# A decoder block in float32: score turns into two banks, slots whose registers are loaded once, and the memory's rows minus their mean on ScalarE

## The chip, the cores and the metric

One core of one Trainium2 chip runs the whole program in one launch. The metric is the device time of that launch in microseconds (us), lower is better. Its engines are TensorE (PE), VectorE (DVE), ScalarE (ACT), GpSimd (POOL) and SyncE (SP). Each runs its own instructions in order, and they wait for each other by semaphores.

## The reference

Two layers over `x` of 16 x 128 x 256, all float32; only the parts that the change touches are spelled out.

```python
x = x + L0_attn(layernorm(x))        # 16 heads of 16: softmax(q k^T / 4) v, then w_o and b_o
x = x + L0_conv(ctx, ctx, layernorm(x), ssm_kernel, D)   # a long convolution per head
x = x + L0_experts(layernorm(x))     # one of 8 experts per row (top 1), and a shared expert
x = x + L1_attn(layernorm(x))        # 16 heads, full attention within each 128 rows
x = x + L1_memory(layernorm(x), ctx, mask)
x = x + L1_ffn(layernorm(x))         # two quantised linear layers

def _layernorm(x, eps=1e-05):
    m = mean(x); v = var(x)
    return (x - m) / sqrt(v + eps)

def L1_memory(h, mem, mask):
    scores = einsum('bsd,bmd->bsm', h, mem) / sqrt(256)
    attn = softmax(where(mask, scores, -1e30))
    return where(any(mask), einsum('bsm,bmd->bsd', attn, mem), 0)

def L0_experts(h, ...):
    e, w = top_1(h @ router.T)
    return sigmoid(w) * glu(h, w1[e], v1[e], w2[e]) + glu(h, shared...)
```

## The kernel before

The rows are cut into 16 tiles of 128 rows x 256 columns, one per batch entry. The stages follow one another: attention of layer 0 with the first steps of the convolution beside it, the convolution, the experts, attention of layer 1 with the memory's cross-attention beside it, and the feed-forward. Each engine's program is written out by hand with counting semaphores; there is no scheduler, so the order in the code is the order on the engine. A function `pipeline` runs a stage's body for t = 0, 1, ..., with the first six t written out, the rest in a loop of two tiles per turn, and the tail written out. What belongs to another stage is put in by `follow(engine, ..., step)`, and the functions `on_act` and `on_dve` of the memory are called so.

**Attention, one body.** TensorE's eight banks are four for the scores `S` (which Q, K and V also use in turn), `T` (bank 4), `O` (bank 5), `M` (bank 6) and `X` (bank 7). For tile t TensorE makes the scores (`pe_scores`, L313) of all 16 heads into `S`; VectorE reduces the first 8 heads to their maximum (L545, "max 0") and subtracts it (L551, "sub 0"), then the same for the other 8 (max 1, sub 1); ScalarE takes the exponential (L468). The probabilities are turned in four groups of four heads (`pe_turn`, L321, turns 0 to 3): four transposes into `T`, and ScalarE copies the bank out (`act_copy`, L473, copies 0 to 3). As `T` is one bank, turn r waits for copy r-1 (semaphore `pT`). Then come P times V (`pe_pv`, L331, into `O`), ScalarE's copy of it, its transposition back into `O` (`pe_o_turn`, L339), and on VectorE the reciprocal of the sums (L568) and the scaled result (L574, "att", semaphore `att`). Layer 0 also turns that result (`pe_att_turn`, L379) and multiplies it by `w_o` (`pe_out`, L386) into `M`; VectorE adds it to x (L581), after GpSimd added the bias to x (L636).

TensorE's order in one body is: scores of t, turn 1 of t-1, (layer 0: the result of t-2), the normed rows of t+1 turned (L250), what follows from convolution or memory, turn 2, (layer 0: `pe_out`), turn 3, Q and K of t+1 (L349, L359), P times V of t-1, turn 0 of t, V of t+1 (L369), `pe_o_turn`. Q may not start before sub 0 has read the scores' banks. The scores wait for ScalarE's copy of V (L485).

**A layer norm.** VectorE takes the statistics of the rows (L216, L221), GpSimd makes 1/sqrt(var + eps) from them (L230, L233), VectorE writes the normed rows (L242, `front_xn`), and TensorE turns them (L250). In layer 0 two of them run per body: that of the next attention tile, and that of the convolution. In layer 1 the second is the memory's.

**The experts.** Rows are sorted by expert; 23 slots of up to 128 sorted rows each belong to one expert. The routing leaves the expert of each slot in a row of SBUF (`expert_of`). The shared expert's second product is L1057, added by VectorE in L1065. Then 12 fill-in products keep TensorE busy (`keep_busy`, L71), and `slots` runs `pe_slot` for each slot: it loads the expert numbers of its own slot and of the slot before from SBUF into registers of TensorE (L1105), turns the rows of the next slot (L1101), turns the hidden layer (L1116) and multiplies by the weights of the expert (L1124 gate and up, L1132 down). The first six slots are written out, the rest lie in a loop.

## Time and profile before

| | us |
|---|---|
| the three runs | 732.82, 733.7, 3345.06 |
| their median | 733.7 |
| the profiled execution | 735.13 |
| its span, first to last instruction | 733.2 |

In the profiled execution TensorE is busy 620.5 us (85% of the span), VectorE 531.9 (73%), ScalarE 386.5 (53%), GpSimd 323.0 (44%), and the mean granted clock of TensorE is 0.956 of full speed. The run of 3345.06 us stands alone and is left aside. The stages as they lie in the trace are: attention of layer 0 until about 175 us, the convolution's products until about 250, the routing, the experts' slots from about 316 to 400, attention of layer 1 from about 411 to 590, the feed-forward to the end. A row of the trace gives the start and the length of an instruction or of several alike in a row; in square brackets stands how long the engine had been idle and what it had waited for.

### The profile page before, as it was taken

Reading aid. Unit: us, or ns where it says so; the run is one execution under the profiler, and the core shown is the slowest. Engines: PE = TensorE matmul, PEld = TensorE weight load, DVE = VectorE, ACT = ScalarE, POOL = GpSimd, SP = SyncE. Lnnn points to the kernel's source line nnn. Section 1 sums busy time; section 2 is a strip of 40 time slices with the busy share of each in tenths; the row PEclk is TensorE's granted clock in tenths of the full one; section 3 lists DMA queues with packets and bytes.
Section 4 is the critical chain, followed back from the end, with each engine's and each line's share of the span. In section 5 each row is a group of like instructions: output and inputs, shape, how many; then the busy total and the mean of one; then the engine's idle time right before and its main releaser. Section 6 shows DMA issues by size and latency. Waiting matters only on the chain.

```text
span 733.2 us, 16347 instructions
## 1 busy us (share of the span) xinstructions
PE 620.5 (85%) x4645; PEld 463.8 (63%) x4647; DVE 531.9 (73%) x1217; ACT 386.5 (53%) x796; POOL 323.0 (44%) x672
## 2 busy tenths in 40 slices
PE   6899999987889899988999777999999667827776
PEld 5787888864444475566777566888887433315554
DVE  4688888873999986325222678899998458779994
ACT  2567777662111123234232264777776438779993
POOL 1223222233999642711111554333333258667772
PEclk9899999999999999999999998999999669969999
DMA  8901400000343100274541213000000000000011
GB/s 302 415 35 31 167 0 0 0 1 6 53 57 57 29 1 0 102 235 132 152 135 50 59 36 109 2 1 0 1 0 1 2 0 1 0 0 1 14 46 57
DMA packets 27342, 42.00 MB, mean 57 GB/s; under 512 B 3520, under 2 KB 22608, under 8 KB 26400
## 3 DMA queue, kind: packets, MB, share of 16 engines
q1 hardware_dynamic: 23808, 31.14, 14.4%
q0 software_dynamic: 3488, 10.28, 4.1%
q8 instruction: 25, 0.41, 0.2%
q14 instruction: 21, 0.17, 0.1%
HBM read 31.15 MB, written 10.26 MB: 56 GB/s over the span
## 4 chain that ended last, share of the span: by engine, by line
PE 61%; issue 12%; ACT 9%; DVE 8%; POOL 5%; DMA 3%; SPq 1%; DVEq 0%; POOLq 0%; ACTq 0%
PE ps L321 9%; PE ps L1124 5%; PE ps L349 5%; PE ps L331 4%; PE ps L313 4%; PE ps L359 4%; PE ps L369 4%; PE ps L713 4%; PE ps L1132 2%; PE ps L386 2%; PE ps L339 2%; POOL sorted_x L1185 2%; ACT wide L473 2%; ACT work L1718 2%; ACT wide L1689 2%
## 5 line engine op out<-in xcount | busy, mean ns | idle before, releaser
L230 POOL TENSOR_TENSOR var_eps<-mv,powers 128x1 f32<-128x1 f32 x80 | 16.8, 209 | 215.2 <-DVE mv L221 215.0
L473 ACT COPY wide<-ps 128x512 f32<-128x512 f32 x128 | 75.1, 587 | 60.9 <-PE ps L321 60.9
L321 PE MATMUL ps<-ident,work 128*128 128x128 f32 x512 | 84.0, 288 | 10.0 <-ACT wide L473 9.0
L545 DVE TENSOR_REDUCE work<-ps 128x8 f32<-128x1024 f32 x64 | 77.9, 1218 | 12.4 <-PE ps L313 12.4
L321 PEld LDWEIGHTS ps<-ident,work 128*128 128x128 f32 x512 | 56.4, 144 | 36.5 <-issue 29.3
L551 DVE TENSOR_TENSOR work<-ps,work 128x1024 f32<-128x1024 f32 x64 | 77.9, 1217 | 0.8 <-issue 0.2
L713 PE MATMUL ps<-ctxT,small 128*128 128x512 f32 (+1 forms) x192 | 65.7, 493 | 8.0 <-DVE ctx_sb L819 3.1
L468 ACT ACTIVATE work<-work 128x1024 f32<-128x1024 f32 x64 | 67.9, 1061 | 8.1 <-DVE work L551 7.5
L713 PEld LDWEIGHTS ps<-ctxT,small 128*128 128x128 f32 x192 | 35.3, 190 | 37.7 <-issue 28.0
L1158 DVE TENSOR_TENSOR work<-work,ps 128x256 f32<-128x256 f32 x23 | 9.7, 421 | 56.6 <-ACT work L1152 56.6
L349 PE MATMUL ps<-xnT,w_qkv 128*128 128x128 f32 x256 | 38.3, 298 | 11.5 <-DVE work L551 9.8
L233 POOL TENSOR_TENSOR rstd<-var_eps,powers 128x1 f32<-128x1 f32 x80 | 44.6, 557 | 6.3
L1168 POOL DMA_DIRECT2D sorted_y<-work x23 | 13.5, 588 | 75.1 <-DVE work L1163 75.1
L1736 PE MATMUL ps<-work,wide 128*128 128x128 f32 x256 | 32.9, 284 | 15.0 <-DVE work L1782 15.0
L216 DVE BATCH_NORM_STATS2 bn<-x 128x6 f32<-128x256 f32 (+1 forms) x96 | 40.5, 422 | 5.2 <-DMA x<-in_x 2.6
L1124 PE MATMUL ps<-wide,work 128*128 x184 | 43.9, 381 | 0.0
L313 PE MATMUL ps<-wide,work 32*128 32x256 f32 x512 | 36.7, 399 | 8.0 <-ACT work L485 6.4
L349 PEld LDWEIGHTS ps<-xnT,w_qkv 128*128 128x128 f32 x256 | 34.3, 208 | 13.4 <-issue 11.5
L833 DVE TENSOR_REDUCE wide<-ctx_sb 128x1024 f32 x32 | 39.0, 1220 | 4.5
L751 ACT COPY xnT<-ps 128x256 f32<-128x256 f32 x32 | 11.8, 373 | 56.9 <-PE ps L713 56.9
L1736 PEld LDWEIGHTS ps<-work,wide 128*128 128x128 f32 x256 | 31.5, 201 | 15.6 <-issue 15.4
L331 PE MATMUL ps<-wide,work 128*32 128x128 f32 x1024 | 35.7, 281 | 2.7 <-ACT wide L473 2.7
(207 smaller groups left out, 1556.5 us busy)
## 6 DMA issues: line engine op xcount, KB each, us to landing
wide<-in_expert_gu SPq DMA_DIRECT2D x1, 4096.0 KB, 20.8
small<-hank SPq DMA_DIRECT2D x32, 128.0 KB, 3.8
sorted_x<-small POOLq DMA_DIRECT2D x1, 2944.0 KB, 12.5
work<-sorted_x SPq DMA_DIRECT2D x23, 128.0 KB, 2.1
sorted_y<-work POOLq DMA_DIRECT2D x23, 128.0 KB, 2.4
xn_all<-in_ctx_rev_t SPq DMA_DIRECT2D x1, 2048.0 KB, 10.7
wide<-in_expert_d SPq DMA_DIRECT2D x1, 2048.0 KB, 25.3
xn_all<-in_ffn_w SPq DMA_DIRECT2D x2, 1024.0 KB, 6.3
```

The lines of the kernel that those rows point to most:

```text
L233: pool.tensor_tensor(f.rstd_v[u], f.var_eps[u], powers[:, 0:1], ALU.pow).then_inc(f.rstd, 1)
L313: mm = pe.matmul(S[i][:, c * 2 * P:(c + 1) * 2 * P], qT[u][rows, c, :], kTm[u][rows, c, :], start=True, stop=True, skip_group_check=True)
L321: mm = pe.transpose(T[:, h * P:(h + 1) * P], prob[r][:, h * P:(h + 1) * P], ident)
L331: mm = pe.matmul(O[VW * k:VW * k + VW, r * P:(r + 1) * P], va[u][:, GH * r + k, :], probT[r][:, k * P:(k + 1) * P], start=True, stop=True, ...
L349: mm = pe.matmul(Q[:, j * P:(j + 1) * P], w[:, c, j * P:(j + 1) * P], xT(c), start=(c == 0), stop=(c == KT - 1), skip_group_check=True)
L468: act.activation(prob2[g], prob2[g], ACT.Exp, scale=ATT_SCALE).then_inc(s["exp"], 1)
L473: act.copy(probT[r], T).then_inc(s["pT"], 1)
L545: dve.tensor_reduce(mxs[:, 8 * g:8 * g + 8], S2[g], AX.X, ALU.max).then_inc(s["mx"], 1)
L551: dve.tensor_tensor(prob2[g].rearrange("p (h k) -> p h k", k=P), S2[g], m.unsqueeze(2).broadcast_to([P, 2 * GH, P]), ALU.subtract).then_in ...
L713: mm = pe.matmul(ps[4 * u + o][:, 0:n], toep[u][:, c, lt * P:(lt + 1) * P], kv[u][:, c, half * UPPER:half * UPPER + n], start=(c == 1 - lt ...
L1124: mm = pe.matmul(ps[2 * k + u][:, 0:NI], xsT[u][:, c * P:(c + 1) * P], w_ex_gu[:, c, ds(expert * (2 * NI) + k * NI, NI)], start=(c == 0), ...
L1736: pe.matmul(TB2[1 - u][:, c * P:(c + 1) * P], y[:, c * P:(c + 1) * P], diag[1 - u], start=(c % 4 == 0), stop=False, skip_group_check=True)
```

## The change

1. **Two banks for turns.** `T` becomes a pair, bank 4 and `O`. Turns 0 and 2 go to bank 4, turns 1 and 3 to `O`. A turn now waits for the copy of the turn two before it, and turn 1 waits instead for the `att` of the tile before, which reads `O`. V of t+1 moves ahead of turn 0 of t. In layer 0, turn 3 comes right behind turn 2, ahead of `pe_out`. In layer 1, turns 2 and 3 come together ahead of the memory's readout and scores; the memory's own turned probabilities go to columns 128 to 255 of `M`, with two waits that this needs, and the wait for `att` ahead of them goes.
2. **VectorE's order.** In layer 1 (and, as the orders below show, in layer 0, where the convolution's normed rows are a step 3 too) step 3 and the memory's maximum come ahead of the reciprocal and `att`.
3. **The memory's norm.** `front_xn` of the memory leaves VectorE. ScalarE writes the mean minus x (Identity, bias the mean, scale -1, step "apart"), behind copy 0. GpSimd makes `nscale`, the reciprocal root times -1/16, and VectorE's score step multiplies by it where it multiplied by 1/16.
4. **The slots.** TensorE loads all 23 expert numbers once, ahead of `keep_busy`, and the 23 slots are all written out.

```diff
-            S, T, O, M, X = ps[0:4], ps[4], ps[5], ps[6], ps[7]
+            S, O, M, X = ps[0:4], ps[5], ps[6], ps[7]
+            T = [ps[4], O]
             def pe_turn(pe, t, u, r):
                 pe.wait_ge(s["exp"], 2 * B + 2 * t + r // 2 + 1)
-                wait(pe, s["pT"], 4 * B + 4 * t + r)
+                if r == 1:
+                    wait(pe, s["att"], B + t)
+                else:
+                    wait(pe, s["pT"], 4 * B + 4 * t + r - 1)
...
-                if there(t):
-                    pe_turn(pe, t, u, 0)
                 if there(t + 1):
                     pe_v(pe, t + 1, 1 - u)
+                if there(t):
+                    pe_turn(pe, t, u, 0)
...
-                wait(pe, s["att"], B + upto(t - 1))
-                follow("pe", pe, t, u, 0, X=X[:, D:2 * D], KO=turned_to(t))
+                follow("pe", pe, t, u, 0, X=X[:, D:2 * D], KO=M)
                 if there(t - 1):
                     pe_turn(pe, t - 1, 1 - u, 2)
+                    pe_turn(pe, t - 1, 1 - u, 3)
                 follow("pe", pe, t, u, 3, KO=M)
                 follow("pe", pe, t, u, 1, KO=M)
-                if there(t - 1):
-                    pe_turn(pe, t - 1, 1 - u, 3)
...
+                follow("act", act, t, u, "apart ready")
                 if there(t):
                     act_copy(act, t, 0)
+                follow("act", act, t, u, "apart")
...
                 follow("dve", dve, t, u, 2, KO=M)
+                follow("dve", dve, t, u, 3, KO=M)
+                follow("dve", dve, t, u, "2 end", KO=M)
                 if there(t - 1):
                     dve_att(dve, t - 1)
-                follow("dve", dve, t, u, "2 end", KO=M)
-                follow("dve", dve, t, u, 3, KO=M)
...
-                load = lambda t: pe.value_load(expert_of[0:1, ds(t, 1)], min_val=0, max_val=NE - 1)
                 if in_range(t):
-                    expert = load(t)
+                    expert = experts[t]
...
                 pe.wait_ge(s["expert"], 1)
+                experts = nc.values_load_multi_w_load_instructions(
+                    expert_of[0:1, :], engines=[mybir.EngineType.PE], min_val=0, max_val=NE - 1)[1]
                 pe.wait_ge(s["sh_h"], 10)
                 pe.wait_ge(s["x_shared"], 2 + DOWN_FIRST)
                 keep_busy(pe, ps[5], ident, 12)
                 pe_turn_slot(pe, 0, 0, 0)
-                slots("pe", pe, pe_slot, 1, 1)
+                for t in range(NS + 1):
+                    pe_slot(pe, t, t % 2, t // 2, experts)
+                    if 2 <= t < 6:
+                        beside_slots("pe", pe, t - 2)
...
                     if there(p):
                         pe.wait_ge(s["exp"], p + 1)
                         wait(pe, s["pT"], p)
-                        pe.transpose(KO, prob[u], ident).then_inc(s["pT_ps"], 1)
+                        wait(pe, s["masked"], upto(t - 3))
+                        wait(pe, s["x_new"], p)
+                        pe.transpose(KO[:, P:2 * P], prob[u], ident).then_inc(s["pT_ps"], 1)
...
+                n = t - 2
+                if step == "apart ready" and there(n):
+                    act.wait_ge(f.stats, f.base + n + 1)
+                    wait(act, f.xnT_ps, f.base + n - 1)
+                if step == "apart" and there(n):
+                    act.activation(slot2(f.xn_buf, u, D), tile_of(x, n), ACT.Identity, bias=f.mean[u],
+                                   scale=-1.0).then_inc(f.xn, 1)
...
-                    dve.scalar_tensor_tensor(sc[1 - u], KO[:, 0:P], float(D) ** -0.5,
+                    dve.scalar_tensor_tensor(sc[1 - u], KO[:, 0:P], nscale[1 - u],
...
-                if step == 3 and there(n):
-                    front_xn(dve, f, n, u)
...
+                    eng.wait_ge(f.rstd, f.base + t - 1)
+                    wait(eng, s["masked"], t - 3)
+                    eng.tensor_tensor(nscale[u], f.rstd_v[u], c_nroot, ALU.mult).then_inc(s["nscale"], 1)
```

TensorE, loop of layer 0's attention, the second half of a body: P times V (L331; behind the change L335), turn 0 (L321; L325), V (L369; L373) and `pe_o_turn` (L339; L343). Before:

```order
L331 MATMUL ps<-wide,work 32x128 [waits att_att,att_v_sb,att_pT]
L331 MATMUL ps<-wide,work 32x128 x15
L318 REGISTER_ALU
L321 MATMUL ps<-ident,work 128x128 [waits att_pT,att_exp]
L321 MATMUL ps<-ident,work 128x128 x3
L369 MATMUL ps<-w_qkv,xnT 128x256 [waits att_sub,att_v_sb]
L369 MATMUL ps<-w_qkv,xnT 128x256
L339 MATMUL ps<-ident,work 128x128 [waits att_oT]
L339 MATMUL ps<-ident,work 128x128 x3
```

With the change:

```order
L335 MATMUL ps<-wide,work 32x128 [waits att_att,att_v_sb,att_pT]
L335 MATMUL ps<-wide,work 32x128 x15
L373 MATMUL ps<-w_qkv,xnT 128x256 [waits att_sub,att_v_sb]
L373 MATMUL ps<-w_qkv,xnT 128x256
L319 REGISTER_ALU
L43 REGISTER_ALU [waits att_exp]
L325 MATMUL ps<-ident,work 128x128 [waits att_pT]
L325 MATMUL ps<-ident,work 128x128 x3
L343 MATMUL ps<-ident,work 128x128 [waits att_oT]
L343 MATMUL ps<-ident,work 128x128 x3
```

V has moved ahead of turn 0, and `pe_o_turn` now follows turn 0 directly.

TensorE, the same loop, the middle of a body: turns 2 and 3 (L321; L325) and `pe_out` (L386; L390). Before:

```order
L43 REGISTER_ALU [waits att_exp]
L321 MATMUL ps<-ident,work 128x128 [waits att_pT]
L321 MATMUL ps<-ident,work 128x128 x3
L386 MATMUL ps<-w_o,work 128x256 [waits att_x_new,att_attT]
L386 MATMUL ps<-w_o,work 128x256
L43 REGISTER_ALU [waits att_exp]
L321 MATMUL ps<-ident,work 128x128 [waits att_pT]
L321 MATMUL ps<-ident,work 128x128 x3
```

With the change:

```order
L43 REGISTER_ALU [waits att_exp]
L325 MATMUL ps<-ident,work 128x128 [waits att_pT]
L325 MATMUL ps<-ident,work 128x128 x3
L43 REGISTER_ALU [waits att_exp]
L325 MATMUL ps<-ident,work 128x128 [waits att_pT]
L325 MATMUL ps<-ident,work 128x128 x3
L390 MATMUL ps<-w_o,work 128x256 [waits att_x_new,att_attT]
L390 MATMUL ps<-w_o,work 128x256
```

The two turns now stand in a row, and `pe_out` behind them.

VectorE, the same loop, the end of a body: the x update (L581; L580), the normed rows of the next attention tile (first L242) and of the convolution (second L242), reciprocal (L568; L567) and `att` (L574; L573). Before:

```order
L581 TENSOR_TENSOR x<-x,ps 128x256
L242 TENSOR_SCALAR xn<-x,mv,rstd 128x256 [waits front0_xnT_ps,front0_rstd]
L568 RECIPROCAL work<-ps 128x16 [waits att_ot_ps]
L574 TENSOR_TENSOR work<-ps,work 128x256 [waits att_attT_ps,att_rsum]
L242 TENSOR_SCALAR work<-x,mv,rstd 128x256 [waits front1_xnT_ps,front1_rstd]
```

With the change:

```order
L580 TENSOR_TENSOR x<-x,ps 128x256
L242 TENSOR_SCALAR xn<-x,mv,rstd 128x256 [waits front0_xnT_ps,front0_rstd]
L242 TENSOR_SCALAR work<-x,mv,rstd 128x256 [waits front1_xnT_ps,front1_rstd]
L567 RECIPROCAL work<-ps 128x16 [waits att_ot_ps]
L573 TENSOR_TENSOR work<-ps,work 128x256 [waits att_attT_ps,att_rsum]
```

The convolution's normed rows now come ahead of the reciprocal and of `att`, straight behind the attention's.

TensorE, between the shared expert (L1057; L1056) and the first slot: fill-in products (L71), turned rows (L1101; L1100), register load (L1105; L1232). Before:

```order
L71 MATMUL ps<-ident 128x128 [waits moe_x_shared,moe_sh_h,moe_expert]
L71 MATMUL ps<-ident 128x128 x11
L1101 MATMUL ps<-ident,work 128x128 [waits moe_xs0]
L1101 MATMUL ps<-ident,work 128x128
L1105 TENSOR_LOAD small
L1105 ISA x2
L1101 MATMUL ps<-ident,work 128x128 [waits moe_xsT,moe_xs1]
L1101 MATMUL ps<-ident,work 128x128
```

With the change:

```order
L1056 MATMUL ps<-w_sh,work 128x256
L1232 TENSOR_LOAD small [waits moe_expert]
L1232 ISA x46
L71 MATMUL ps<-ident 128x128 [waits moe_x_shared,moe_sh_h]
L71 MATMUL ps<-ident 128x128 x11
L1100 MATMUL ps<-ident,work 128x128 [waits moe_xs0]
L1100 MATMUL ps<-ident,work 128x128
```

All registers are now loaded, and 46 register instructions run, ahead of the fill-in products.

## Rows read from the trace of the kernel before

**Rows 1.** The page, part 4: the chain that ended last, by engine.
```profile
PE 61%; issue 12%; ACT 9%; DVE 8%; POOL 5%; DMA 3%; SPq 1%; DVEq 0%; POOLq 0%; ACTq 0%
```

**Rows 2.** Timeline, TensorE, a tile of layer 0 (start us, length us, operation, count).
```profile
90.59 1.15 PE L313 MATMUL ps<-wide,work 32*128 32x256 f32 x16 [0.21 <-ACT work L485]
...
93.00 0.65 PE L321 MATMUL ps<-ident,work 128*128 128x128 f32 x4
...
94.50 0.60 PE L321 MATMUL ps<-ident,work 128*128 128x128 f32 x4
94.93 1.06 PE L349 MATMUL ps<-xnT,w_qkv 128*128 128x128 f32 x8
...
99.18 0.60 PE L339 MATMUL ps<-ident,work 128*128 128x128 f32 x4
```

**Rows 3.** Timeline, VectorE, the same tile.
```profile
91.80 1.22 DVE L545 TENSOR_REDUCE work<-ps 128x8 f32<-128x1024 f32 x1 [0.34 <-PE ps L313]
...
93.28 1.21 DVE L551 TENSOR_TENSOR work<-ps,work 128x1024 f32<-128x1024 f32 x1
...
99.82 0.26 DVE L568 RECIPROCAL work<-ps 128x16 f32<-128x16 f32 x1 [0.70 <-PE ps L339]
...
100.45 0.40 DVE L242 TENSOR_SCALAR work<-x,mv,rstd 128x256 f32 x1
```

**Rows 4.** Timeline, ScalarE, then GpSimd, the same tile.
```profile
92.36 0.58 ACT L473 COPY wide<-ps 128x512 f32<-128x512 f32 x1 [1.52 <-PE ps L321]
...
99.22 0.73 POOL L636 TENSOR_TENSOR x<-x,row_bias 128x256 f32 x1
```

**Rows 5.** Timeline, TensorE: scores, tiles 1, 15 (layer 0); 4, 15 (layer 1).
```profile
24.55 1.15 PE L313 MATMUL ps<-wide,work 32*128 32x256 f32 x16 [0.66 <-ACT work L485]
...
156.47 1.15 PE L313 MATMUL ps<-wide,work 32*128 32x256 f32 x16 [0.23 <-ACT work L485]
...
460.99 1.15 PE L313 MATMUL ps<-wide,work 32*128 32x256 f32 x16 [0.23 <-ACT work L485]
...
563.39 0.93 PE L313 MATMUL ps<-wide,work 32*128 32x256 f32 x12 [0.23 <-ACT work L485]
```

**Rows 6.** Timeline, GpSimd and VectorE, in layer 0 and behind it.
```profile
62.27 0.74 POOL L636 TENSOR_TENSOR x<-x,row_bias 128x256 f32<-128x256 f32 x1
...
62.78 0.40 DVE L242 TENSOR_SCALAR work<-x,mv,rstd 128x256 f32<-128x256 f32 x1
...
165.50 1.24 DVE L242 TENSOR_SCALAR work<-x,mv,rstd 128x256 f32<-128x256 f32 x1
```

**Rows 7.** Line L1105, TensorE's queue, 334.4 to 336 us (ns min/median/max); timeline.
```profile
L1105 PEldq TENSOR_LOAD <-small x2: 296/304/313, 334.6 to 335.2; - x2
L1105 PEldq FUSED_REGOPS  x2: 146/148/151, 334.9 to 335.6; - x2
...
313.18 2.92 PE L71 MATMUL ps<-ident 128*128 128x128 f32 x24 [0.71 <-DVE x L1065]
...
335.97 0.30 PE L1101 MATMUL ps<-ident,work 128*128 128x128 f32 x1 [1.06 <-issue]
```

**Rows 8.** Timeline, TensorE: the slots.
```profile
347.53 1.92 PE L1124 MATMUL ps<-wide,work 128*128 x8
...
391.86 1.93 PE L1124 MATMUL ps<-wide,work 128*128 x8
...
394.99 1.93 PE L1124 MATMUL ps<-wide,work 128*128 x8
```

**Rows 9.** Busy us (count) PE, PEld, DVE, ACT, POOL; PEclk, DMA, GB/s.
```profile
440.00:442.50 2.50, 0.00 (x0) 0.00 (x0) 2.50 (x4) 0.04 (x2) 1.89 (x3) 0.50 0.73 234
442.50:446.00 3.50, 3.41 (x16) 3.44 (x16) 2.34 (x4) 2.36 (x4) 2.15 (x4) 0.50 0.93 352
```

**Rows 10.** Timeline, TensorE, behind layer 1's last tile.
```profile
575.40 1.09 PE L321 MATMUL ps<-ident,work 128*128 128x128 f32 x4 [1.13 <-ACT wide L473]
...
585.00 0.66 PE L250 MATMUL ps<-ident,work 128*128 128x128 f32 x2 [1.52 <-DVE work L242]
```

40 lines of the change are left out of this document (21 added, 19 removed).

## The prediction

> **What bounds the kernel now.** I read the chain of waits first. By engine its shares are TensorE 61%, issue 12%, ScalarE 9%, VectorE 8% [rows 1]: the span is set by TensorE for the most part, and what can be won is short waits of TensorE on the others. So next I read one tile of layer 0 on every engine. The scores start at 90.59, Q at 94.93, `pe_o_turn` at 99.18 and, after a wait of 0.21 for ScalarE's V copy, the next scores about 0.8 behind it [rows 2]. Three things hold TensorE up there. The scores wait for V. Turn 2 starts at 93.00 right behind copy 1, which runs from 92.36 for 0.58 [rows 2, 4]. And Q comes behind turn 3, which waits its turn behind `pe_out` and copy 2. The reader is to see that all are a few tenths; the tile takes 9.42 us (24.55 to 156.47 is 131.92 for 14 tiles), and in layer 1 9.31 (460.99 to 563.39 is 102.40 for 11) [rows 5].
>
> **Layer 0.** With two banks and the new order the three waits go, and I ask what is late next.
>
> *TensorE and sub 0.* Max 0 starts 1.21 behind the scores, sub 0 at 93.28 and ends at 94.49, so 3.90 behind the scores' start [rows 2, 3]. With 0.14 for the semaphore, Q can start at 4.04, against 4.34 now. TensorE's own work up to there is 4.34 less the two waits, about 0.3, so 4.05: the same. Q to `pe_o_turn` is 4.25 [rows 2] and only changes its order. `pe_o_turn` takes 0.43 before the next instruction can follow, as turn 3 does ahead of Q (94.50 to 94.93), plus 0.03. The sum is 4.05 + 4.25 + 0.46 = 8.76.
>
> *VectorE and GpSimd.* The attention's next normed rows are made late in the body, in step with GpSimd, which starts adding the bias (L636) at 99.22, when it has made the convolution's 1/sqrt; that is 7.42 behind max 0 at 91.80 [rows 3, 4]. Only now may the convolution's normed rows (L242) start, and the change puts them ahead of the reciprocal. They need 0.35 on the queue, reciprocal and `att` need 0.63 (99.82 to 100.45) [rows 3], so max 0 of the next tile may come 7.42 + 0.08 + 0.35 + 0.63 = 8.48 behind the last. Taken alone that is below 8.76. But L242 now starts with L636 beside it, where before it came when L636 was over. What this costs the rows bound from both sides: L242 at 62.78 had L636 (62.27, 0.74) beside it for half its time and took its usual 0.40; at 165.50, with GpSimd starting an addition at the same time, it took 1.24 [rows 6]. The nearest row is in between, as L242 would start some 0.1 into L636; I take half of the 0.84, 0.42, which gives 8.90, and keep 8.76 (cost hidden behind TensorE) and 9.32 for the range.
>
> So a tile takes 8.90 where it took 9.42, and 14 tiles save 7.3. The two ends of the stage have the same waits in smaller number, 1.1 together (an estimate: two tiles' worth of 0.52). Layer 0 gives **8.4** (bounds 14 x 0.10 = 1.4 and 16 x 0.66 = 10.6).
>
> The Trainium skill, GPSIMD Engine Reference, section Specifications, says that GpSimd shares its interfaces to SBUF with VectorE, and that the two get in each other's way where VectorE runs in a mode that uses both ports or reads two inputs from SBUF. By that rule taken hard, L242 would take its 1.24 here each time and the gain of layer 0 would be near its lower bound. The row at 165.50 agrees; the one at 62.78 shows no delay.
>
> The added wait of turn 1 for `att` stands with the scores of the next tile behind it: turn 1 comes 1.08 behind the scores' start, `att` about 0.1 before that by the sum above. I cost it at nothing; each tenth by which `att` is later costs a tenth per tile.
>
> **Layer 1.** The memory's normed rows leave VectorE (0.40 a tile) and go to ScalarE. There they stand behind copy 0, in a stretch where ScalarE has room: it is busy 53% of the span. The multiplication for `nscale` is one more small step of GpSimd. Here no L242 stands beside L636, so TensorE's sum of 8.76 should hold; turns 2 and 3 go ahead of the memory's products, and the wait for `att` is gone. 11 tiles save 11 x (9.31 - 8.76) = 6.1. The four tiles at the start of the layer have the same turns, 4 x 0.6 = 2.4. Behind the last tile TensorE waits 1.13 for a copy ahead of a turn at 575.40 and 1.52 for the normed rows at 585.00 [rows 10]. Two banks remove most of the first, ScalarE's earlier rows most of the second, and the rest of the tail has some smaller ones of the first kind: I take 3.3, from 1 to 4. Layer 1 gives **11.8** (7 to 13). The lower bound is that the tile stays bound by VectorE, whose work a tile lost only 0.40: 11 x 0.40 + 1 + 1.6.
>
> **The slots.** What goes: two loads per slot on TensorE's queue, each 0.30 for the load and 0.15 for the operation behind it [rows 7]. A slot takes 3.41 in the middle ((391.86 - 347.53) / 13), while the last, with no load of a next slot, takes 3.13 [rows 8]. Not all of the difference is the loads; I take 0.21 a slot for 13 slots, 2.7. The one place where the issue itself shows, 1.06 of idle ahead of 335.97 [rows 7], goes too, and some 0.3 elsewhere: 4.1 in all (1 to 5).
>
> What comes: one load and 23 pairs of register operations ahead of the fill-in products. In the trace two such pairs start 0.7 apart, 0.30 of it the load between them [rows 7]. So a pair needs 0.3 to 0.4, and no less than 0.15; 23 x 0.30 + 0.3 = 7.2, with ends at 3.8 and 9.7. TensorE ends its product at 312.47 (313.18 less 0.71), and its queue is free about one us earlier. The fill-in products now start at 318.5 in place of 313.18, 5.3 later; the first slot stands behind them, and nothing covers this. And the array is idle for 6 us. After a shorter idle time (440.00 to 442.50 has no product at all) the granted clock was 0.50 for the next 3.5 us of work [rows 9], which is the lower of the two levels, 1.2 GHz; the work of these 3.5 us takes twice its time, which loses 1.8. The prologue costs 7.1, from 2.3 (short operations, no fall of the clock) to 10.5. The slots lose **3.0** net.
>
> The Trainium skill, TensorE: Matmul & The Clock Gate, Part 1, says that an array left idle falls back to 1.2 GHz and needs sustained work to come back. The rows at 440.00 and 442.50 agree. If the clock didn't fall here, the sum would be 1.8 lower.
>
> **Sum.** 8.4 + 11.8 - 3.0 = 17.2 less. The profiled execution would take 735.13 - 17.2 = 717.9. The median of the runs shown is 1.4 below it, which gives 716.5; I say **717**.
>
> **Rivals.**
>
> 1. *The loads cost next to nothing.* If the register operations overlap the shared expert's last products, the slots gain 4 in place of losing 3, and the time is 716.5 - 7.1 = 709.5. For it: TensorE's queue runs ahead of the array. Against it: it can do so by one group of products only, and 0.15 is a measured duration of the operation.
> 2. *VectorE and GpSimd take the gain of layer 0.* L242 at the full 1.24, or `att` late for turn 1, holds the tile at 9.32. Layer 0 then gives 1.4 + 1, about 6 less: 722.5. With layer 1 at its lower bound too it is 727. For it: the row at 165.50, and that VectorE is busy 73% over the whole. Against it: the row at 62.78.
> 3. *Slower than before: the slots written out.* Their code is now a straight run on TensorE's queue with 23 different bodies. If each needed fetching as at 335.97, where the array sat idle 1.06 on issue behind new code [rows 7], 20 slots would cost 21, and the time would be 716.5 + 21, about 738. It decides against the change from 0.85 us per slot on. Against it: the first six slots are written out already, and issue shows once.
> 4. *The change doesn't do what it says.* Turns in two banks still wait, since ScalarE's copies come in the same order and Q waits for sub 0. Then the layers give 0.1 a tile, some 5 with the tail, and with the slots' loss the time is 731.
>
> **How the numbers follow.** My forecast, with its own range of 713 to 720, has 0.48; rival 1 has 0.12, rival 2 0.28, rival 3 0.04, rival 4 0.08. The range from 710 to 726 leaves out the last two and a part of the first two. About 2% is what a measurement of this kernel can tell from no change, so the border to "faster" is at 719.0. Below it lie rival 1 and most of the forecast's own range, 0.57; within 2% lie the rest of it, rivals 2 and 4, 0.38; slower is rival 3 and little else, 0.05.
>
> **What would show it.** In the profile after, the start of the scores of tile 1 to that of tile 15 in layer 0 should be about 124.6 in place of 131.9, with L242 at a mean between 0.4 and 0.8 us, and the wait ahead of the scores gone. In layer 1 the tile should take 8.8. Ahead of the slots the register operations should fill some 7 us, the fill-in products should start near 318.5 at a granted clock of 0.5 and last nearly 5 us; the slots should be 3.1 to 3.3 apart. I am wrong if the register operations run faster than 0.2 a pair, if L242 is never stretched, or always, or if a new wait for `att` stands ahead of turn 1.

## The result, and the profile after

| | before | with the change |
|---|---|---|
| median of 14 runs each, us | 734.48 | 728.98 |
| ratio to before | | 0.9925 (95% interval 0.9901 to 0.995) |
| profiled execution, its span, us | 735.13, 733.2 | 725.95, 724.3 |

The change gains 0.75%, 5.5 us, where 717 was predicted and 710 to 726 was the range. The run of 3345.06 us stays aside. The profiled execution of the changed kernel is one of the quickest of its 14, so its span is 8.9 lower than that of before; what follows reads where these 8.9 lie.

The page's chain of waits, by engine, reads now:

```profile
PE 56%; issue 15%; DVE 14%; ACT 7%; DMA 3%; POOL 3%; DVEq 1%; SPq 1%; POOLq 0%; ACTq 0%
```

VectorE has 14% of it where it had 8%, and issue 15% where it had 12% [rows 1]; both turn up again below. Next the starts of the scores in the timeline of TensorE (scores are L314 now), tiles 1 and 15 of layer 0, 4 and 15 of layer 1, to be held against [rows 5]:

```profile
20.80 0.93 PE L314 MATMUL ps<-wide,work 32*128 32x256 f32 x12 [0.23 <-ACT work L482]
...
146.91 1.15 PE L314 MATMUL ps<-wide,work 32*128 32x256 f32 x16
...
457.80 1.15 PE L314 MATMUL ps<-wide,work 32*128 32x256 f32 x16
...
556.23 1.14 PE L314 MATMUL ps<-wide,work 32*128 32x256 f32 x15
```

Layer 0: 20.80 to 146.91 is 126.11 for 14 tiles, 9.01 each, against 131.92. The waits on ScalarE ahead of the scores are gone. Layer 1: 98.43 for 11 tiles, 8.95 each, against 102.40. So the loops alone give 5.8 + 4.0.

The last products of the convolution, first before, then with the change, end at 250.80 and at 238.50:

```profile
246.67 4.13 PE L713 MATMUL ps<-ctxT,small 128*128 128x512 f32 x12 [0.19 <-POOL ctxT L773]
...
233.74 4.76 PE L712 MATMUL ps<-ctxT,small 128*128 128x256 f32 x14
```

Of these 12.3 the loop of layer 0 gives 5.8, and from the scores of tile 15 to the end of the convolution it is 2.7 less. The other 3.75 lie ahead of tile 1, and they are for the most part the clock's. TensorE waits 2.52 for sub 0 of tile 0 in both kernels, and its next eight products, Q of tile 1, take 2.05 before and 1.13 with the change:

```profile
17.73 2.05 PE L349 MATMUL ps<-xnT,w_qkv 128*128 128x128 f32 x8 [2.52 <-DVE work L551]
...
16.64 1.13 PE L353 MATMUL ps<-xnT,w_qkv 128*128 128x128 f32 x8 [2.52 <-DVE work L550]
```

From 18 to 20 us the granted clock is 0.50 before, its lower level of 1.2 GHz, and 1.00 with the change. It doesn't go with the kernel: in another profile of the changed kernel (changed_again, below) it is 0.50 there too, and tile 1 starts at 23.89.

Then the stretch ahead of the slots. The first rows are the operations of the new line L1232 on TensorE's queue (ns min/median/max, first and last start), then the timeline:

```profile
L1232 PEldq FUSED_REGOPS  x23: 146/146/165, 305.4 to 311.7; - x23
...
L1232 PEldq TENSOR_LOAD <-small x1: 6018/6018/6018, 299.3 to 299.3; - x1
...
294.82 5.60 PE L1056 MATMUL ps<-w_sh,work 128*128 128x256 f32 x24 [0.20 <-DVE x L1064]
312.11 4.48 PE L71 MATMUL ps<-ident 128*128 128x128 f32 x24 [11.69 <-issue]
```

The one load of 23 registers took 6.02 us, and the 23 pairs behind it run from 305.4 to 312. TensorE ends the shared expert's products at 300.42 (294.82 and 5.60) and is idle for 11.69. It was idle for 0.71 before [rows 7]. The fill-in products then take 4.48 instead of 2.92. The stretches show why:

```profile
312.00:316.40 4.40, 4.29 (x24) 4.32 (x25) 0.00 (x0) 0.00 (x0) 0.00 (x0) 0.61 0.00 0
```

Behind the counts of the five engines stands the granted clock: it is 0.61 on average over these 4.4 us, and 1.00 behind them. So it was at its lower level, 1.2 GHz, for most of them. By the Trainium skill, TensorE: Matmul & The Clock Gate, Part 1, an idle array falls back to half its rate; the trace agrees. The first slot's gate product starts at 317.61, where it started at 317.54 before, although the convolution's last product had ended 12.3 us earlier. **All that the profile had gained up to there is gone at this place.** The slots give back a little:

```profile
317.61 1.89 PE L1122 MATMUL ps<-wide,work 128*128 x8
...
391.81 1.92 PE L1122 MATMUL ps<-wide,work 128*128 x8
```

From the first to the last gate product it is 74.20, against 77.45 before: 3.3 less.

### The profile page after: what moved, and what is told of

The parts are those of the page before. It is cut to its first block, busy times and chain, and to the rows that moved or that the text cites. A ratio compares the mean times of both kernels' runs of the same rounds, so it can differ in the third digit from the quotient of the medians.

```text
span 724.3 us, 16265 instructions
## 1 busy us (share of the span) xinstructions
PE 610.9 (84%) x4646; PEld 464.7 (64%) x4646; DVE 532.9 (74%) x1201; ACT 395.2 (55%) x812; POOL 320.9 (44%) x688
## 4 chain that ended last, share of the span: by engine, by line
PE 56%; issue 15%; DVE 14%; ACT 7%; DMA 3%; POOL 3%; DVEq 1%; SPq 1%; POOLq 0%; ACTq 0%
PE ps L325 6%; PE ps L1122 5%; PE ps L353 4%; PE ps L373 4%; PE ps L712 4%; PE ps L363 4%; PE ps L335 4%; PE ps L1003 3%; PE ps L314 3%; PE ps L1130 2%; DVE work L550 2%; DVE work L544 2%; PE ps L1056 2%; ACT work L1735 2%; ACT wide L1706 2%
## 5 line engine op out<-in xcount | busy, mean ns | idle before, releaser
L325 PE MATMUL ps<-ident,work 128*128 128x128 f32 x512 | 75.6, 279 | 5.3 <-DVE work L573 3.7
L550 DVE TENSOR_TENSOR work<-ps,work 128x1024 f32<-128x1024 f32 x64 | 77.8, 1216 | 0.6
L325 PEld LDWEIGHTS ps<-ident,work 128*128 128x128 f32 x512 | 59.0, 143 | 21.0 <-issue 15.7
L1166 POOL DMA_DIRECT2D sorted_y<-work x23 | 12.5, 545 | 84.9 <-DVE work L1161 84.9
L750 ACT COPY xnT<-ps 128x256 f32<-128x256 f32 x32 | 11.8, 373 | 56.6 <-PE ps L712 54.9
L314 PE MATMUL ps<-wide,work 32*128 32x256 f32 x512 | 36.7, 400 | 2.1 <-ACT work L482 1.1
L373 PE MATMUL ps<-w_qkv,xnT 128*128 128x256 f32 x128 | 37.3, 416 | 0.4 <-DVE work L550 0.4
```

The lines of the kernel that those rows point to most:

```text
L314: mm = pe.matmul(S[i][:, c * 2 * P:(c + 1) * 2 * P], qT[u][rows, c, :], kTm[u][rows, c, :], start=True, stop=True, skip_group_check=True)
L325: mm = pe.transpose(T[r % 2][:, h * P:(h + 1) * P], prob[r][:, h * P:(h + 1) * P], ident)
L373: mm = pe.matmul(V[:, 0:D], xT(c), w[:, c, 2 * D:3 * D], start=(c == 0), stop=(c == KT - 1), skip_group_check=True)
L550: dve.tensor_tensor(prob2[g].rearrange("p (h k) -> p h k", k=P), S2[g], m.unsqueeze(2).broadcast_to([P, 2 * GH, P]), ALU.subtract).then_in ...
```

## The experiments

They ran on two chips, before_again, slots_only, one_bank and best on one, the others on another. On both the kernel before takes some 746 us (745.75 to 746.73) in place of 734.5, so each kernel is read by its ratio to the kernel before on the same chip, and a ratio times 734.5 makes it comparable with the prediction. In the table, 'tile' is the start of scores to start of scores, layer 0 over 14 intervals from tile 1 to 15, layer 1 over 11 from tile 4 to 15, from each profile; 'slots' is from the first to the last gate product. The tiles of kernels with the same code agree within 0.01 from profile to profile. The slots don't: their first 8 intervals, where the other parts of the stage run beside them, take 29.9 to 31.8 us in the seven profiles with the old slots and 28.3 to 31.4 in the four with all numbers loaded ahead. The last 14 intervals take 3.37 to 3.41 each with the old slots and 3.21 with every kind of slots written out.

| kernel | ratio (95% interval) | us | tile, layer 0 | tile, layer 1 | slots |
|---|---|---|---|---|---|
| before (profile of before_again) | 1 | 746 | 9.42 | 9.31 | 77.1 |
| changed_again | 0.9926 (0.9899 to 0.9952) | 740.97 | 9.01 | 8.95 | 76.4 |
| slots_as_before | 0.9805 (0.9763 to 0.9848) | 731.39 | 9.01 | 8.95 | 79.0 |
| no_bounds_check | 0.9826 (0.9783 to 0.9868) | 731.83 | 9.01 | 8.95 | 74.0 |
| half_ahead | 0.9821 (0.9781 to 0.9862) | 732.15 | 9.01 | 8.95 | 73.9 |
| once_in_slot | 0.9747 (0.9681 to 0.9813) | 727.93 | 9.01 | 8.95 | 73.8 |
| turns_only | 0.9852 (0.9799 to 0.9905) | 734.97 | 8.94 | 9.26 | 77.7 |
| order_undone | 0.9813 (0.9763 to 0.9863) | 732.14 | 8.94 | 9.01 | 78.9 |
| norm_undone | 0.9843 (0.9793 to 0.9893) | 735.37 | 9.01 | 9.14 | 77.8 |
| slots_only | 1.0101 (1.0072 to 1.013) | 754.06 | 9.43 | 9.31 | 73.2 |
| one_bank | 1.0162 (1.0117 to 1.0207) | 758.84 | 9.92 | 10.00 | 78.1 |
| best | 0.9781 (0.9754 to 0.9809) | 730.63 | 8.94 | 8.95 | 74.3 |

### The registers

**slots_as_before.** The changed kernel with the old slots:

```diff
-                experts = nc.values_load_multi_w_load_instructions(
-                    expert_of[0:1, :], engines=[mybir.EngineType.PE], min_val=0, max_val=NE - 1)[1]
...
+                load = lambda t: pe.value_load(expert_of[0:1, ds(t, 1)], min_val=0, max_val=NE - 1)
+                    expert = load(t)
+                    expert_y = load(t - 1)
```

> The changed kernel with its slots and their register loads as they were before; the attention parts of the change stay. Theory (the register prologue eats what the earlier stages gave): the trace of the changed kernel has one load of 6.02 us and 46 register operations of 6.5 us ahead of the fill-in products, and TensorE idle for 11.7 us; without them the first slot's products start at about 305.5 instead of 317.6, the slots take 79.4 again instead of 76.1, and the time is about 9 us below the changed kernel's 729.0, so 720. Rival (the slots couldn't start earlier anyway, for the sorted rows or the code come late): the first slot stays near 317 and the time near 729 to 732.

First slots_as_before, then changed_again, the changed kernel on the same chip:

```profile
294.96 1.89 PE L1056 MATMUL ps<-w_sh,work 128*128 128x256 f32 x8
312.01 2.92 PE L71 MATMUL ps<-ident 128*128 128x128 f32 x24 [0.71 <-DVE x L1064]
315.94 1.89 PE L1123 MATMUL ps<-wide,work 128*128 x8
...
297.32 1.89 PE L1056 MATMUL ps<-w_sh,work 128*128 128x256 f32 x8
324.73 0.55 PE L71 MATMUL ps<-ident 128*128 128x128 f32 x1 [10.22 <-issue]
```

The ratio is 0.9805, which is 720.2 on the first chip: the theory's number. The first slot didn't start at 305.5 here but at 315.9, with a wait that is shown below under before_again; the changed kernel has that wait too. From the shared expert's second products to the first gate product the changed kernel takes 32.7 (297.3 to 330.0) and this one 21.0 (295.0 to 315.9). The difference, 11.7, is what the registers cost, the fallen clock included.

**no_bounds_check.** The same load without the 46 operations:

```diff
-                    expert_of[0:1, :], engines=[mybir.EngineType.PE], min_val=0, max_val=NE - 1)[1]
+                    expert_of[0:1, :], engines=[mybir.EngineType.PE], min_val=0, max_val=NE - 1,
+                    skip_runtime_bounds_check_because="expert_of counts thresholds, 0 to NE - 1")[1]
```

> The changed kernel without the 46 register operations (the check of each number against its bounds) behind the one load. Theory (load and operations add up on TensorE's queue, 6.0 and 6.5 us): the idle time ahead of the fill-in products falls from 11.7 to about 5.2, time about 722.5. Rival (the load alone is what is waited for, the operations run beside it or are cheap): time above 727.

```profile
L1232 PEldq TENSOR_LOAD <-small x1: 5614/5614/5614, 308.1 to 308.1; - x1
...
303.66 6.30 PE L1056 MATMUL ps<-w_sh,work 128*128 128x256 f32 x16 [5.22 <-DVE x L1064]
313.93 5.42 PE L71 MATMUL ps<-ident 128*128 128x128 f32 x24 [3.96 <-issue]
```

The ratio 0.9826 is 721.7, near the 722.5 of the theory. The idle time fell from 10.2 (changed_again, same chip) to 3.96. Load and operations add up. The clock fell behind the shorter idle time as well: it was 0.51 on average over the 5.37 us of work behind it, and the fill-in products took 5.42.

**half_ahead.** Twelve numbers ahead, the rest in their slots:

```diff
+                    if t >= 12:
+                        experts[t] = pe.value_load(expert_of[0:1, ds(t, 1)], min_val=0, max_val=NE - 1)
...
-                experts = nc.values_load_multi_w_load_instructions(
-                    expert_of[0:1, :], engines=[mybir.EngineType.PE], min_val=0, max_val=NE - 1)[1]
+                experts = dict(enumerate(nc.values_load_multi_w_load_instructions(
+                    expert_of[0:1, 0:12], engines=[mybir.EngineType.PE], min_val=0, max_val=NE - 1)[1]))
```

> The changed kernel with 12 numbers loaded ahead of the slots, the other 11 one by one in their slots. Theory (a load costs some 0.26 us per register, 6.02 / 23): the one load takes 3.1 us, the 24 operations behind it 3.4, the idle time falls by some 6.0, time 723. Rival (a load of several registers has a fixed price of some 6 us): load still 6, time 726.

```profile
L1234 PEldq FUSED_REGOPS  x12: 146/146/165, 312.1 to 315.3; - x12
...
L1234 PEldq TENSOR_LOAD <-small x1: 3057/3057/3057, 308.9 to 308.9; - x1
...
L1106 PEldq TENSOR_LOAD <-small x11: 297/301/319, 362.0 to 394.0; - x11
```

12 registers took 3.06 us, 0.255 each; 23 took 5.61 to 6.02, 0.24 to 0.26 each; one alone takes 0.30. The theory of a price per register holds, the fixed price is refuted. The ratio 0.9821 gives 721.3, somewhat better than the 723 expected.

**once_in_slot.** Nothing ahead, each slot loads its own number once:

```diff
                 if in_range(t):
-                    expert = experts[t]
+                    expert = experts[t] = pe.value_load(expert_of[0:1, ds(t, 1)], min_val=0,
+                                                        max_val=NE - 1)
...
-                experts = nc.values_load_multi_w_load_instructions(
-                    expert_of[0:1, :], engines=[mybir.EngineType.PE], min_val=0, max_val=NE - 1)[1]
+                experts = {}
```

> The changed kernel with the slots still written out, but each slot loading its own number once (23 single loads, none ahead). Theory: no idle time ahead of the fill-in products, first slot at about 305.5; half of the register work of before per slot hides behind the products, so that a slot takes 3.2 on average: time 729.0 - 12.1 = 717, some 3 below the kernel with the slots as before. Rival (the single load in each slot costs the same as two did, since its latency stands at the head of each slot): no better than the kernel with the slots as before, 720.

The ratio 0.9747 gives 715.9, the theory's 717 within the interval. But the interval, 0.9681 to 0.9813, also holds the 0.9805 of slots_as_before, so the times alone don't decide against the rival; the slots do. They take 73.8 us against 79.0 with the old slots, as short as with all numbers ahead (74.0 in no_bounds_check), and nothing is paid ahead of them. Of the 5.2 some 2.9 lie in the first 8 intervals, where profiles of the same code differ by as much; the last 14 took 3.21 in place of 3.37 each.

This gain can't be put down to the second load, because the loop went with it. The old slots' loop, kernel before, two of its slots per turn:

```profile
347.04 0.43 PE L1101 MATMUL ps<-ident,work 128*128 128x128 f32 x2 [0.33 <-issue]
...
350.25 0.43 PE L1101 MATMUL ps<-ident,work 128*128 128x128 f32 x2
...
353.96 0.43 PE L1101 MATMUL ps<-ident,work 128*128 128x128 f32 x2 [0.35 <-issue]
```

TensorE waits on issue once per turn of the loop. Within a turn the gate products of slots_as_before start 3.26 to 3.29 apart with two loads per slot, against 3.29 with one or none; across the turn it is 3.5 to 3.7 against 3.12. In the slots ahead of the loop, which are written out with both loads, three intervals are 3.09 to 3.11, as they are without any load. Between the fifth and the sixth of these slots the loads do show: 5.41 or more with two, 4.77 with one, 4.21 with none. Whether the turn of the loop or the loads right behind it make the difference across the turn is not shown; slots written out with two loads each, or a loop with one, would tell, and were not run.

**slots_only.** The kernel before with this part of the change alone (the diff is that of part 4).

> The kernel before with the fourth part of the change alone: registers loaded ahead of the fill-in products, slots written out. Theory: 12.1 us of prologue and fallen clock against 3.3 gained in the slots, so 8.8 slower than the kernel before, ratio 1.012. Rival (the part's price hangs on the earlier stages being faster): ratio 1.00 to 1.005.

The ratio is 1.0101, 7.4 us by 734.5: the theory's 1.012 lies within the interval. The part by itself makes the kernel slower, and it costs what was read from the changed kernel: against before_again, on the same chip, it takes 12.5 us more from the shared expert's second products to the first gate product and 3.9 less in the slots.

### The attention

**changed_again** repeats the changed kernel beside the others.

> The changed kernel itself, unaltered, beside the next three on one chip. The runs of slots_as_before and once_in_slot stood on a chip where the kernel before took 745.75 and where TensorE, behind the first of the shared expert's second products, waited up to 5 us on issue, which the two profiles of the first chip don't show. Theory: the ratio to the kernel before is 0.9925 as measured, if that wait comes alike in both kernels. Rival: the changed kernel suffers more from it, and the ratio is over 1.

0.9926 again: the result doesn't hang on the chip.

**turns_only, order_undone and norm_undone** are the changed kernel with the old slots. In addition order_undone has VectorE's order as before, norm_undone the memory's norm, and turns_only both. The two edits, the second in part:

```diff
                 follow("dve", dve, t, u, 2, KO=M)
-                follow("dve", dve, t, u, 3, KO=M)
-                follow("dve", dve, t, u, "2 end", KO=M)
                 if there(t - 1):
                     dve_att(dve, t - 1)
+                follow("dve", dve, t, u, "2 end", KO=M)
+                follow("dve", dve, t, u, 3, KO=M)
...
-                if step == "apart" and there(n):
-                    act.activation(slot2(f.xn_buf, u, D), tile_of(x, n), ACT.Identity, bias=f.mean[u],
-                                   scale=-1.0).then_inc(f.xn, 1)
+                if step == 3 and there(n):
+                    front_xn(dve, f, n, u)
```

> Of the change only the two banks and TensorE's order stay; VectorE's order, the memory's norm and the slots are those before. Theory: in layer 0 the tile is then bound by TensorE and sub 0 as summed, 8.76, or somewhat above, and the convolution's L242 takes 0.40 again; in layer 1 VectorE's chain (max 0 to max 0 with 0.33 more of L242) holds the tile at 9.2 or more. Ratio to the kernel before about 0.985. Rival: VectorE's order is what lets the tile shrink, and layer 0 stays at 9.2 or above.

> The changed kernel with the slots as before and VectorE's order as before (att ahead of step 3 and of the memory's maximum). Theory: the new order is worth nothing in layer 0, since VectorE waits for the reciprocal's input anyway and L242 takes 0.75 in the new place and 0.40 in the old; the tile is 8.8 to 9.0 either way. In layer 1 att comes 0.28 earlier for turn 1, and the maximum later: 8.95 within 0.1. Ratio as slots_as_before, 0.98. Rival: a tile of 9.2 or more in either layer.

> The changed kernel with the slots as before and the memory's normed rows by VectorE again (the scale 1/16 on the scores, no nscale). Theory: only layer 1 changes; VectorE has 0.33 more on its queue per tile, and its tile goes from 8.95 to about 9.2: 3 us for the stage, ratio 0.984. Rival (the tile of 8.95 is TensorE's, VectorE has room): no change in the stage, 0.980.

With slots_as_before these are four corners of a square, and their tiles separate the parts. Layer 0: 8.94 with the old order, 9.01 with the new, whatever the norm. So the two banks and TensorE's order gain 0.48 per tile, and VectorE's new order costs 0.07. Layer 1: the banks alone give 0.05 per tile (9.31 to 9.26); the norm on ScalarE gives 0.25 with the old order and 0.19 with the new; the order gives 0.12 and 0.06. My theory for turns_only holds in layer 1, 9.2 or more for VectorE's chain (9.26); in layer 0 it had 8.76 or somewhat above, and 8.94 is 0.18 above; that of order_undone holds, with 9.01 in layer 1 within the 0.1; of norm_undone I had 9.2 and measured 9.14. The ratios, 0.9852, 0.9813 and 0.9843, are as expected, but their intervals overlap, and the reading rests on the tiles.

The timeline shows what the new order costs in layer 0. Changed kernel, VectorE (L242 into `work` is the convolution's), then GpSimd, then TensorE:

```profile
101.82 0.82 DVE L242 TENSOR_SCALAR work<-x,mv,rstd 128x256 f32 x1 [0.18 <-POOL rstd L233]
...
102.83 0.42 DVE L573 TENSOR_TENSOR work<-ps,work 128x256 f32<-128x256 f32 x1
103.35 1.22 DVE L544 TENSOR_REDUCE work<-ps 128x8 f32<-128x1024 f32 x1
...
104.83 1.21 DVE L550 TENSOR_TENSOR work<-ps,work 128x1024 f32<-128x1024 f32 x1
...
101.76 0.73 POOL L635 TENSOR_TENSOR x<-x,row_bias 128x256 f32 x1
...
103.40 0.63 PE L325 MATMUL ps<-ident,work 128*128 128x128 f32 x4
```

L242 takes 0.82 with L635 (the bias) starting beside it, and `att` (L573) ends at 103.25; turn 1 starts at 103.40, 1.26 behind the scores (102.14), where it takes 1.07 without a wait (511.47 to 512.54 in layer 1): 0.19 of waiting. For the eleven of the convolution's L242 between 56 and 147 us the mean is 0.825 in the changed kernel, 0.48 before. In eight tiles of the loop in a row (75.05 to 137.66) they take 0.71 to 0.86, mean 0.77; among the rest are one of 1.39 and one of 0.41.

The Trainium skill, GPSIMD Engine Reference, section Specifications, says that GpSimd shares its interfaces to SBUF with VectorE, with contention where VectorE runs in a two-port mode or reads two inputs from SBUF. The trace agrees that VectorE is delayed where the two meet, L242 by 0.3 to 0.5 in these tiles, while the bias keeps its 0.73; which of the page's two conditions holds for L242 no run here shows.

**one_bank.** All turns in one bank again, under the new orders and with the old slots:

```diff
-            T = [ps[4], O]
+            T = [ps[4], ps[4]]
...
-                if r == 1:
-                    wait(pe, s["att"], B + t)
-                else:
-                    wait(pe, s["pT"], 4 * B + 4 * t + r - 1)
+                wait(pe, s["pT"], 4 * B + 4 * t + r)
```

> The changed kernel with the slots as before and all turns in one bank again, each waiting for the copy ahead of it; the new order on TensorE and on VectorE and the memory's norm on ScalarE stay. Theory (the second bank is what lets turn 3 follow turn 2): turn 3 now waits some 0.7 for copy 2 ahead of everything behind it; layer 0's tile goes from 8.95 to 9.5, layer 1's likewise, ratio 0.996. Rival (the order, V ahead of turn 0 above all, made the gain): the tiles stay under 9.1.

Worse than expected: 9.92 and 10.00 a tile where I had 9.5, ratio 1.0162 where I had 0.996. The direction is the theory's, the rival (the order made the gain) is refuted: under the new order the second bank is worth 0.9 to 1.05 a tile, and the new orders with one bank cost 0.5 in layer 0 and 0.7 in layer 1 against the kernel before. So the order alone doesn't gain. Whether the second bank would gain under the old order was not run.

### What remained

**before_again**, for a profile of the kernel before where it takes 746 us:

> The kernel before, unaltered, for a profile on the chip of the other runs. Theory: it too waits up to 5 us on issue within the shared expert's second products (L1057) while GpSimd sends off its 16 scatters, and this is where most of the 12 us lie by which the kernel before is slower there (746 against 734.5). Rival: it doesn't, the wait belongs to the changed kernels, and its other stages are longer all over.

```profile
304.89 1.89 PE L1057 MATMUL ps<-w_sh,work 128*128 128x256 f32 x8
306.98 1.10 PE L1057 MATMUL ps<-w_sh,work 128*128 128x256 f32 x4 [0.19 <-issue]
312.62 2.04 PE L1057 MATMUL ps<-w_sh,work 128*128 128x256 f32 x4 [4.53 <-DVE x L1065]
316.14 5.92 PE L1057 MATMUL ps<-w_sh,work 128*128 128x256 f32 x16 [1.48 <-DVE x L1065]
322.77 2.47 PE L71 MATMUL ps<-ident 128*128 128x128 f32 x20 [0.71 <-DVE x L1065]
```

The second products begin at 304.89 as on the first chip (304.78) and the fill-in products at 322.77 in place of 313.18. The 9.6 between are most of the 13.3 by which the two spans differ (746.5 and 733.2). Most of the rest lies in the first four tiles of layer 1, which took 49.6 here and 45.5 on the first chip; the changed kernel takes 47.0 there in changed_again. The profiles of the kernels on the other chip of the experiments show such waits in the same place (slots_as_before: 3.14 on issue). The kernel before has them as well, on VectorE and on issue, in the time in which GpSimd sends off its scatters. That they hang on these scatters was not tried; that they don't come from the change is shown.

**best.** Two banks, the norm on ScalarE, each number loaded once in its slot, and the old order of VectorE in layer 0:

```diff
                 follow("dve", dve, t, u, 2, KO=M)
+                if layer == 0 and there(t - 1):
+                    dve_att(dve, t - 1)
                 follow("dve", dve, t, u, 3, KO=M)
                 follow("dve", dve, t, u, "2 end", KO=M)
-                if there(t - 1):
+                if layer == 1 and there(t - 1):
                     dve_att(dve, t - 1)
```

> Two banks, the memory's norm on ScalarE, the slots written out with each number loaded once in its slot, VectorE's new order in layer 1 alone (att ahead of the convolution's rows in layer 0 again). Theory: the sum of the single results: once_in_slot's 0.9747 less 1.0 us for the order in layer 0, ratio 0.973. Rival (layer 0's gain is lost in what follows): 0.975 or above.

The tiles are the expected ones, 8.94 and 8.95, and so are the slots. The ratio, 0.9781, is the rival's by its number, and the 0.973 of the theory lies outside the interval. But the intervals of best and once_in_slot overlap, and the two profiles differ where their code doesn't: from the start of the last scores to the end once_in_slot took 165.2 and best 168.1, the other kernels with two banks 167.3 to 168.4. In the first 39 us of this stretch, up to 600, the granted clock was 0.78 in once_in_slot and 0.69 in best. So best and once_in_slot can't be told apart by time, and neither can be told from slots_as_before (0.9805, 0.9763 to 0.9848). Both beat the changed kernel: 0.9781 and 0.9747 against 0.9926, with intervals apart.

## Why the prediction was wrong

Two terms of the sum were mis-sized. The register prologue was to cost 7.1 and cost 12.1, 5.0 more. Layer 1 was to give 11.8 and gave 5.7, 6.1 less. Added to the 717, either miss alone would have left the time in the range (722 or 723); the two together took it out.

**The register prologue** is the step whose price was wrong. I wrote "one load and 23 pairs", took 0.30 for the load from [rows 7], and made 7.2 of it with 9.7 as the upper end. The pairs were right: 23 took 6.5 by the trace, 0.28 each, where I had 0.30. The load was not: a load of 23 registers is one instruction in the program but took 6.02 us, 0.26 per register, twenty times the row of a load of one. The row that I priced it with was of another size, and I had not bounded it by 23 such rows, 6.9, which would have given 13.8 for the whole. The idle time was 11.7 (predicted about 6), and the fill-in products took 4.48 against 2.92, 1.6 more (predicted 1.8). In all the first slot lost 12.1 against the stage ahead of it, where I had 7.1.

**The slots** gained 3.3 in the first pair of profiles, in the term's range of 1 to 5 (4.1 taken): intervals of 3.12 and 3.29 in turn, as said (3.1 to 3.3). Against before_again it is 0.8 (changed_again) and 3.9 (slots_only), for the first intervals spread. The mechanism was wrong in part: I put 0.21 a slot down to the two loads, but within a turn of the loop two loads cost nothing, and the difference lies across the turn. Net the fourth part cost 8.8 in the profile, 7.4 by slots_only, where I had 3.0.

**Layer 0.** The tile came out at 9.01 (8.90 predicted), L242 at 0.825, or 0.77 in the steady tiles (0.82 predicted, between the ends 0.40 and 1.24). The row of 1.24 was of another kind, though: beside it GpSimd ran an instruction of 1.04 (L768), not the bias's 0.73. The loop gave 5.8, predicted 7.3. That the attention to the last product of the convolution took 12.3 less in the profile, not 8.4, lies with the two ends, where I had 1.1 for both: 2.7 behind tile 15, and the 3.75 ahead of tile 1, which are luck of the profile and not the change's. Tile 1 starts anywhere from 20.3 to 24.6 in the twelve profiles of the experiments, and at 20.9 with the attention untouched (slots_only), where the granted clock didn't fall either. The wait of turn 1 for `att`, costed at nothing, took 0.19 a tile, as the sentence about each tenth had it; with VectorE's old order the tile is 8.94. This wait, and an L242 that is stretched in each tile of the loop from 75.05 on, stood on my list of signs that I am wrong, and both came.

**Layer 1.** I had 8.76 a tile from TensorE's sum and no rival ring; it was 8.95, and 4.0 in place of 6.1. The 8.95 is a mean of two kinds of tile. The first, with TensorE from its scores to the next:

```profile
502.59 1.15 PE L314 MATMUL ps<-wide,work 32*128 32x256 f32 x16
...
506.54 1.16 PE L353 MATMUL ps<-xnT,w_qkv 128*128 128x128 f32 x8
...
510.94 0.60 PE L343 MATMUL ps<-ident,work 128*128 128x128 f32 x4
511.47 1.15 PE L314 MATMUL ps<-wide,work 32*128 32x256 f32 x16
```

This tile takes 8.88, without a wait of TensorE. Scores to Q are 3.95, Q to `pe_o_turn` 4.40, `pe_o_turn` to scores 0.53; my sum had 4.05, 4.25 and 0.46. I had said that Q to `pe_o_turn` only changes its order, but in the new order it is 0.15 longer. In layer 0 turns_only shows the same sum, 3.96, 4.38 and 0.53, and its steady tile is 8.88 too, so this term was 0.12 short in both layers. The second kind takes 9.13 to 9.16 and comes once per turn of the loop of two tiles. There a ring that I missed goes through both engines. VectorE, then TensorE:

```profile
511.57 0.26 DVE L567 RECIPROCAL work<-ps 128x16 f32<-128x16 f32 x1 [0.25 <-PE ps L343]
511.87 0.42 DVE L573 TENSOR_TENSOR work<-ps,work 128x256 f32<-128x256 f32 x1
512.55 0.48 DVE L1395 SCALAR_TENSOR_TENSOR x<-ps,mem_cols,x 128x256 f32 x1 [0.26 <-issue]
512.95 1.21 DVE L544 TENSOR_REDUCE work<-ps 128x8 f32<-128x1024 f32 x1
...
514.42 1.21 DVE L550 TENSOR_TENSOR work<-ps,work 128x1024 f32<-128x1024 f32 x1
...
515.68 1.16 PE L353 MATMUL ps<-xnT,w_qkv 128*128 128x128 f32 x8 [0.18 <-DVE work L550]
...
520.07 0.60 PE L343 MATMUL ps<-ident,work 128*128 128x128 f32 x4
```

`pe_o_turn` (L343) releases the reciprocal, behind it come `att`, the memory's update of x (L1395), max 0 and sub 0, and sub 0 releases Q, from which it is 4.39 to the next `pe_o_turn`. Max 0 starts 1.48 behind the scores (511.47), not 1.21, since the memory's update of x stands ahead of it and is itself late: VectorE is idle for 0.26 between `att` and L1395, and in the chain of waits register operations of its queue stand there, among them those of the loop's own line (L59). In the tile of 8.88 L1395 follows `att` without a gap, at 503.33, and max 0 comes 1.21 behind the scores. Where VectorE has the normed rows as well (turns_only, 9.30) every tile of the loop is longer.

Of layer 1's start I expected 2.4 and got nothing: the first four tiles took 45.53 against 45.54. There VectorE has the experts' sum and two conversions of 1.2 us each ahead of max 0, and TensorE waits for sub 0, before and after, in the changed kernel for 4.89 at once:

```profile
439.15 2.04 PE L353 MATMUL ps<-xnT,w_qkv 128*128 128x128 f32 x8 [4.89 <-DVE work L550]
```

My own [rows 9] lay in this stretch; I used them for the clock and didn't ask what had made TensorE idle there. The tail gave 1.75 of 3.3: the copies' waits went, and ones for ScalarE's L488 (2.10 at 563.94) and for `att` (0.90 at 565.49) came. Layer 1 in all gave 5.7, below the 7 of its lower bound.

**The rivals.** Rival 1, cheap loads, is refuted. Rival 2 asked for L242 at its full 1.24 and a tile of 9.32; it wasn't so, although L242 was stretched as forecast. Rival 3, code that is written out being slow to fetch, is refuted by once_in_slot and slots_only, which have the same straight run and among the shortest slots. Rival 4 had the layers give 0.1 a tile; they gave 0.41 and 0.36, and one_bank shows that the second bank is needed for it. No case held a dearer prologue, or a layer 1 that gives less than 7.

Three small slips in my working change nothing of this: 4 x 0.6 for layer 1's start should have been 4 x 0.55, 2.2; 23 pairs at 0.4 with a load of 0.3 make 9.5, not 9.7; and a prologue of 7.2 from 311.47 on ends at 318.7, not 318.5.

The sum with the measured terms, from the two profiles: 12.3 (to the end of the convolution) - 12.1 - 0.3 (between the convolution and the fill-in) + 3.3 + 4.0 + 1.75 = 8.9, the difference of the spans. The medians differ by 5.5. Without the 3.75 ahead of tile 1, where the clock fell in one profile and not in the other, the sum is 5.2. The changed kernel's 14 runs fall in two groups, seven from 725.86 to 727.25 with a mean granted clock of 0.949 to 0.953 and seven from 728.95 to 731.78 with 0.944 to 0.947; its two profiles, one with the fallen clock ahead of tile 1 and one without, differ there by 3.1. That this is what parts the groups is likely but not shown, as no run of the second group has a profile.

## What to carry to other kernels

An instruction that moves n values is priced by n, from the row of one, before it is written down as one; and what is hoisted out of a loop in which it hides behind other work must be paid in full at the place to which it goes. Here one load in each slot left the slots as short as none, while all of them together cost 12 us of an idle TensorE and a fallen clock. Before a limit is taken from one engine's sum, follow the ring of waits through both engines once around, with every instruction that stands on the queues in between, the loop's own register operations among them. And when two things change at once, here the loads and the loop, the gain belongs to neither until one is tried without the other.

## What the hardware showed

- One register load of n values: 0.30 us for 1, 3.06 for 12, 5.61 to 6.02 for 23.
- A register operation and its check took 0.28 us from one to the next on TensorE's queue, though they are shown at 0.146 and 0.018.
- VectorE's L242, 0.40 alone, took 0.71 to 0.86 when GpSimd's addition of a bias (0.73) had started 0.01 to 0.16 before it, and 0.40 to 0.43 when that was 0.5 before. Beside a GpSimd instruction of 1.04 that started 0.05 behind it, it took 1.24.
- Behind 11.7 us of idle time TensorE's granted clock averaged 0.61 over the next 4.4 us of work, behind 3.96 us (no_bounds_check) 0.51 over the next 5.4. Behind 2.5 us at the start of the program it fell to 0.50 in some profiles (before, changed_again) and stayed at 1.00 in another (after).
- A loop of two bodies per turn showed once per turn: TensorE waited 0.33 to 0.35 on issue in the old slots, VectorE 0.26 in layer 1's attention.
- The same kernel took 1.6% more on two other chips. In the one profile of the kernel before from there 9.6 of 13.3 us lie in one place, where TensorE waited on issue and on VectorE for up to 4.5 us at once.
